# A mixture-of-experts feed-forward: the order of transposes and down products in each group

## The chip, the cores and the metric

The kernel runs on one core of a Trainium2 chip. The metric is the device time of one execution in microseconds. The kernel before takes 568.52 us, the median of three runs (567.76 to 568.71).

## The reference

The input x has shape (8, 256, 128). The first part is causal attention with 16 query heads of 8 columns and one key and value head, rotary tables, a bias, a residual and a layer norm. The second part is an RMS norm, causal attention with 16 query and 4 key heads of 64 columns, a residual, and then a mixture of experts, whose output is added and layer-normed:

```
logits = xf @ router_w + router_b
vals, idx = top_k(logits, 2);  scores = softmax(vals)
oh = one_hot(idx, 8);  pos = cumsum(cumsum(oh, axis=0), axis=1)
emask = oh * (pos < 256);  m = max over both choices of the admitted expert
h = gelu((xf @ w2[m]) * (xf @ w1[m]))        # 256 hidden columns
y = h @ w3[m]
slot = y where the choice was admitted, else xf
out = sum over the two choices of slot * scores
```

Each of the 2048 tokens so goes through one expert alone, m.

## The kernel before, in words

The batch of 8 is run as a software pipeline of steps; the last steps route the tokens. Tokens are handled in two passes: tiles 0 to 9 (five batch entries) and tiles 10 to 15. In each pass VectorE works out a slot for every token so that the tokens of an expert lie together (`slots`, L1713), GpSimd scatters the rows to `xs_dram` by indirect DMAs (`scatter`, L605) and loads the slots back as tiles of 128 rows (`load_slots`). A pass has 17 or 13 such tiles, each of one expert; they are worked in **16 groups** of two tiles (groups 8 and 15 have one). For group n:

- TensorE turns the slots into bank "xg" of the ring (`turn_slots`, L1211, recorded at L1218). ScalarE copies them to xT_a or xT_b by the group's parity (`take_slots`, L2136, recorded at L2140).
- TensorE forms both up products (`up`, L1236, recorded at L1242) into ps_st. Expert numbers are loaded to registers for two groups at a time (`find_experts`, L1223).
- ScalarE copies one half (`copy`, L2145, L2151, tile prod), VectorE multiplies it by the other (`gate`, L1750, L1756), ScalarE does the gelu (`gelu`, L2153, L2159).
- TensorE turns the gelu's rows into bank "ht" (`turn_hidden`, L1246, recorded at L1252), VectorE copies them to hidT, which the profile names pvs (`take_hidden`, L1759, L1763).
- TensorE forms the down product into bank "dn" (`down`, L1255, recorded at L1262; its w3 has the name pvb), VectorE copies it to ysb, which the profile names qkr (`take_outputs`, L1766, L1771), and SP stores that to `ys_dram` (L557).

When the stores of a pass have landed, GpSimd gathers the rows per token (`gather`, L630, recorded at L632), and VectorE adds them with their weights (`add_outputs`, L1782, recorded at L1792), forms statistics (L1799) and normalises. In the last group VectorE adds the first five tiles of the first pass right after its copies.

The groups overlap by an order written out by hand for each engine. In the loop's turn n TensorE forms the up product of n, and then, before the change, turns the gelu's rows of n-1, turns the slots of n+1 and forms the down product of n-2. VectorE gates n, copies the hidden rows of n-1 and then the outputs of n-2. ScalarE does the copy of n, the slots of n+1, the gelu of n. The routing of the second pass goes in between (`between`, both engines, by the table BETWEEN).

Four PSUM banks form a ring. `Ring.__init__` lists every use of a bank in TensorE's order; a use waits (`fill`) until the use four places earlier was emptied, and a reader waits (`filled`) until the counter `full` has reached the use's number:

```
def bank(self, step, name):
    return self.at[step, name] % self.banks
def full(self, step, name):
    return self.at[step, name] + 1
def freed(self, step, name):
    return self.at[step, name] // self.banks
```

So the list in `Ring.__init__` and TensorE's own order must agree. `down(n)` waits for `take_hidden(n)`; `turn_hidden(n)` waits for `gelu(n)`; `up(n)` waits for `take_slots(n)` and for the gate of n-2; `take_outputs(n)` waits for the down product and for the store of n-2, which has the same half of ysb.

Of the kernel before, what the change touches and what calls it, by code (L numbers as in the profile page):

```python
# [32 lines left out]
NB, T, C = 8, 256, 128  # L33
# [18 lines left out]
GROUPS = [(i, list(range(START[i] + k, START[i] + min(k + 2, COUNT[i])))) for i in range(2) for k in range(0, COUNT[i], 2)]  # L52
NG = len(GROUPS)
# [47 lines left out]
BETWEEN = {(0, 0): [(NB - 1, "xfT")], (0, 1): [(NB, "xfT"), (NB - 1, "lg"), (NB, "lg")],  # L101
           (1, 1): [(NB, "cnt1")], (2, 0): [(NB, "rk1")]}


def stages(step):

    return {x for x, a in AHEAD.items() if 0 <= step + a < NB} - ({"MA"} if step < FIRST + 4 else set())


class Ring:  # L110
# [3 lines left out]
    def __init__(self, banks):  # L114
        self.banks, self.at = banks, {}
        for step in range(FIRST, NB):
            for at, name in OPENING.get(step, []):
                self.add(at, name)
            for stage, name in ORDER if step not in OPENING else []:
                if stage in stages(step):  # L120
                    for at, n in IN_STEP.get(step, {}).get(name, [(step, name)]):
                        self.add(at, n)
        for n in range(NG + 1):
            for at, name in BETWEEN.get((n, 0), []) + [(NB, f"ht{n - 1}")] * (n > 0) \
                    + [(NB, f"xg{n + 1}")] * (n + 1 < NG) + [(NB, f"dn{n - 2}")] * (n > 1) + BETWEEN.get((n, 1), []):
                self.add(at, name)
        self.add(NB, f"dn{NG - 1}")

# [78 lines left out]
def build(nc, x, Wq, bq, Wk, bk, Wv, bv, Wo, bo, g1, g2, wq, wk, wv, wo, router_w, router_b,  # L207
          w1, w2, w3, cf, cb, out):
    with ExitStack() as ctx:
# [31 lines left out]
        down = cft[:, CF_DOWN:CF_DOWN + E]  # L241
# [219 lines left out]
        def emptied(eng, s, name):  # L461

            eng.wait_ge(free[RING.bank(s, name)], RING.freed(s, name) + 1)
# [232 lines left out]
        def _(pe):  # L696
            order = iter(RING.at)

            def fill(s, name):

                assert next(order) == (s, name)
                b, f = RING.bank(s, name), RING.freed(s, name)
                if f > 0:
                    pe.wait_ge(free[b], f)
                return ps_r[:, b, :]
# [169 lines left out]
            def turn_tokens(s):  # L875

                o = fill(s, "xfT")
                pe.wait_ge(xf_in, s)
                for t in range(NT):
                    mm = nc.tensor.transpose(o[:, P * t:P * (t + 1)], xf[:, t, :], ident)  # L880
                mm.then_inc(full, 1)
# [11 lines left out]
            def counts(part):  # L893

                lo, hi = PARTS[part]
                pe.wait_ge(oh_in, part + 1)
                fill(ROUTED[part], f"cnt{part}")
                o = counted(part)
                nc.tensor.matmul(o, tri, oh_b[:, 0:2, lo:hi, :], start=True, stop=False, skip_group_check=True)
                for i in range(hi - 1):  # L900
                    first = max(lo, i + 1)
                    mm = nc.tensor.matmul(o[:, :, first - lo:, :], cbt[:, CB_ONES:CB_ONES + P],
                                          oh_b[:, 0:2, i, :].unsqueeze(2).broadcast_to([P, 2, hi - first, E]),
                                          start=False, stop=i == hi - 2, skip_group_check=True)
                mm.then_inc(full, 1)

            def ranks(i):

                lo, hi = PASSES[i]
                pe.wait_ge(ch_in, i + 1)  # L910
                fill(ROUTED[i], f"rk{i}")
                o = ranked(i)
                nc.tensor.matmul(o[:, 0:hi - lo, :], tri, chosen[:, lo:hi, :], start=True, stop=False,
                                 skip_group_check=True)
                for k in range(lo, hi):
                    mm = nc.tensor.matmul(o[:, k - lo + 1:, :], cbt[:, CB_ONES:CB_ONES + P],
                                          chosen[:, k, :].unsqueeze(1).broadcast_to([P, hi - k, E]),
                                          start=False, stop=k == hi - 1, skip_group_check=True)
                mm.then_inc(full, 1)
# [326 lines left out]
            def turn_hidden(n, g):  # L1246

                pe.wait_ge(hid_in, n + 1)
                o = fill(NB, f"ht{n}").rearrange("p (t k c) -> p t k c", t=2, k=HK)
                for t in range(len(g)):  # L1250
                    for k in range(HK):
                        mm = nc.tensor.transpose(o[:, t, k, :], hid[:, n % 2, t, P * k:P * (k + 1)], ident)  # L1252
                mm.then_inc(full, 1)

            def down(n, g):  # L1255

                emptied(pe, NB, f"ht{n}")
                o = fill(NB, f"dn{n}")
                for t, tile in enumerate(g):
                    at = expert.pop(tile)  # L1260
                    for k in range(HK):
                        mm = nc.tensor.matmul(o[:, C * t:C * (t + 1)], hidT[:, n % 2, t, k, :],  # L1262
                                              w3_flat[:, bass.ds(at + C * k, C)], start=k == 0, stop=k == HK - 1)
                mm.then_inc(full, 1)

            def between(n, half):

                for at, name in BETWEEN.get((n, half), []):
                    if name == "cnt1":
                        counts(1)  # L1270
                    if name == "rk1":
                        ranks(1)
                    if name == "xfT":
                        turn_tokens(at)
                    if name == "lg":
                        logits(at)
# [4 lines left out]
            for n, (i, g) in enumerate(GROUPS):  # L1281
                up(n, i, g)
                if n % 2:
                    find_experts(n + 1)
                between(n, 0)
                if n > 0:
                    turn_hidden(n - 1, GROUPS[n - 1][1])
                if n + 1 < NG:
                    turn_slots(n + 1, *GROUPS[n + 1])
                if n > 1:  # L1290
                    down(n - 2, GROUPS[n - 2][1])
                between(n, 1)
            turn_hidden(NG - 1, GROUPS[NG - 1][1])
            down(NG - 2, GROUPS[NG - 2][1])
            down(NG - 1, GROUPS[NG - 1][1])


# [1 line left out]
        def _(dve):  # L1299
# [313 lines left out]
            at = [0]  # L1613
# [145 lines left out]
            def take_hidden(n, g):  # L1759

                b = filled(dve, NB, f"ht{n}")
                w = len(g) * HID
                V.tensor_copy(hidT[:, n % 2].rearrange("p t k c -> p (t k c)")[:, 0:w], ps_r[:, b, 0:w]) \  # L1763
                    .then_inc(free[b], 1)

            def take_outputs(n, g):  # L1766

                b = filled(dve, NB, f"dn{n}")
                if n > 1:
                    dve.wait_ge(ys_dma[n % 2], 16 * (n // 2))  # L1770
                V.tensor_copy(ysb[:, n % 2, 0:len(g), :], ps_r[:, b, 0:len(g) * C].rearrange("p (t c) -> p t c", c=C)) \  # L1771
                    .then_inc(free[b], 1)
# [53 lines left out]
            def between(n, half):  # L1826

                if (n, half) == (0, 1):
                    take_logits(NB - 1, NB - 2)
                    take_logits(NB, NB - 1)  # L1830
                    first_choices(1)
                if (n, half) == (1, 1):
                    admit(1)
                if (n, half) == (2, 0):
                    slots(1)
                if (n, half) == (8, 1):
                    shares(*PASSES[1], 2)
                if (n, half) == (10, 1):
                    dve.wait_ge(z_in, NB)
                    add_kept(0, 5, 1)  # L1840
                if (n, half) == (11, 1):
                    add_kept(5, 10, 1)
                if (n, half) == (12, 1):
                    add_kept(10, 16, 3)
                if (n, half) == (15, 1):
                    add_outputs(0)
# [11 lines left out]
            for n, (i, g) in enumerate(GROUPS):  # L1858
                gate(n, g)
                between(n, 0)  # L1860
                if n > 0:
                    take_hidden(n - 1, GROUPS[n - 1][1])
                if n > 1:
                    take_outputs(n - 2, GROUPS[n - 2][1])
                between(n, 1)
            take_hidden(NG - 1, GROUPS[NG - 1][1])
            take_outputs(NG - 2, GROUPS[NG - 2][1])
            statistics(0)
            take_outputs(NG - 1, GROUPS[NG - 1][1])
            add_outputs(1)  # L1870
# [337 lines left out]
```

## Time and profile before

| | |
|---|---|
| median of three runs | 568.52 us |
| the profiled execution | 569.94 us |
| its span, first to last instruction | 568.1 us |
| TensorE matmul busy | 474.3 us (83%) |
| VectorE busy | 373.4 us (66%) |
| ScalarE busy | 231.3 us (41%) |
| GpSimd busy | 161.9 us (28%) |
| mean granted TensorE clock | 0.957 of full |

The groups of the feed-forward lie between 481 and 549 us of the span; what comes after is the last store, six gathers, the sums and the final layer norm. PE is TensorE's matmul, DVE is VectorE, ACT is ScalarE, POOL is GpSimd. A busy share says little of a stage with several limits, so the timelines of the single engines are what to read here. The ends of matmuls are modelled by the profiler, and successive ones overlap; the starts give the pace.

### The profile page before, as it was taken

The page shows a single profiled execution, that of the slowest core. Times are in us where ns is not written, and L with a number is a line of the kernel's source. Part 1 is how long each engine was busy: PE and PEld are TensorE (multiplying, and loading weights), DVE is VectorE, ACT ScalarE, POOL GpSimd, SP SyncE. Part 2 cuts the span into 40 slices and gives each one's busy share as a digit, 9 for nine tenths or more (in the row PEclk, how much of TensorE's full clock was granted, in tenths as well). Part 3 has the DMA queues.
Part 4 walks back from the last instruction along what each step waited for, and adds up shares of the span by engine and source line. Part 5 has one row for each costly group of instructions (what it writes and reads, how often), then busy time and mean ns, then how long its engine had stood idle before and what let it go on. Part 6 is the DMA issues. An engine that isn't in the chain of part 4 may idle for free.

```text
span 568.1 us, 8434 instructions
## 1 busy us (share of the span) xinstructions
PE 474.3 (83%) x2980; PEld 262.4 (46%) x2980; DVE 373.4 (66%) x1023; ACT 231.3 (41%) x418; POOL 161.9 (28%) x200
## 2 busy tenths in 40 slices
PE   3877877899899999999998999899888689798730
PEld 2445443454455455536454554455436236465520
DVE  3634789667666786585867577776966136745585
ACT  1252431744554274338334642642431330545332
POOL 4311222402402243033313132232332760051612
PEclk9986999999999999999999999999988789999985
DMA  7400000000030003001100300030430350041213
GB/s 213 168 2 2 1 2 1 2 1 1 3 77 2 0 3 77 1 3 36 42 1 4 76 2 0 5 76 1 141 86 10 106 161 1 1 133 32 64 53 97
DMA packets 19095, 23.95 MB, mean 42 GB/s; under 512 B 2630, under 2 KB 15374, under 8 KB 18158
## 3 DMA queue, kind: packets, MB, share of 16 engines
q1 hardware_dynamic: 15308, 18.29, 11.9%
q0 software_dynamic: 1648, 4.07, 2.6%
q10 hardware_dynamic: 2098, 1.05, 0.6%
q8 instruction: 25, 0.41, 0.3%
q14 instruction: 16, 0.13, 0.1%
HBM read 16.81 MB, written 6.28 MB: 41 GB/s over the span
## 4 chain that ended last, share of the span: by engine, by line
PE 57%; DVE 19%; ACT 11%; issue 6%; POOL 3%; another core or an unknown queue 2%; DMA 1%; ACTq 1%; POOLq 0%; DVEq 0%
PE ps_r L997 6%; PE ps_st L962 6%; PE ps_r L867 5%; DVE rmax_a L1340 4%; ACT pt L1902 4%; PE ps_r L712 4%; PE ps_r L1024 4%; PE ps_st L1242 4%; PE ps_st L951 4%; PE ps_r L1013 3%; PE ps_r L770 3%; DVE rmax L1340 3%; PE ps_r L844 2%; POOL qkr L603 2%
## 5 line engine op out<-in xcount | busy, mean ns | idle before, releaser
L603 POOL TENSOR_TENSOR qkr<-qkr,prod 128x512 f32<-128x512 f32 (+1 forms) x48 | 52.3, 1095 | 191.6 <-DVE prod L1466 190.5
L1340 DVE TENSOR_REDUCE rmax_a<-ps_r 128x2 f32<-128x512 f32 (+1 forms) x96 | 61.2, 686 | 31.2 <-PE ps_r L844 31.0
L1340 DVE TENSOR_REDUCE rmax<-ps_r 128x2 f32<-128x512 f32 (+1 forms) x96 | 60.7, 684 | 13.5 <-PE ps_r L976 13.1
L1902 ACT ACTIVATE pt<-ps_st 128x1024 f32<-128x1024 f32 x48 | 46.5, 1022 | 54.7 <-PE ps_st L754 54.6
L712 PE MATMUL ps_r<-cbt 128*128 128x256 bf16 (+1 forms) x192 | 61.9, 323 | 4.0 <-ACT xT_b L1926 1.1
L1911 ACT ACTIVATE pt<-ps_st 128x1024 f32<-128x1024 f32 x48 | 47.3, 1022 | 37.0 <-PE ps_st L962 31.6
L997 PE MATMUL ps_r<-pt,vb 128*64 128x512 f32 x192 | 50.0, 627 | 7.7 <-issue 4.2
L640 POOL TENSOR_TENSOR oT<-pvb,oT 128x1024 f32<-128x1024 f32 x14 | 32.9, 2371 | 78.9 <-DMA oT<-inv_dram 78.9
L1024 PE MATMUL ps_r<-wqkv,xT_b 128*128 128x512 f32 x96 | 44.5, 600 | 4.3 <-DVE rmax_a L1340 3.5
L712 PEld LDWEIGHTS ps_r<-cbt 128*128 128x128 bf16 x192 | 18.6, 97 | 48.0 <-issue 34.6
L962 PE MATMUL ps_st<-qbuf,kbuf 64*128 64x512 f32 x288 | 39.8, 408 | 0.0
L844 PE MATMUL ps_r<-kq_a 128*128 128x512 f32 x84 | 39.2, 532 | 0.0
L1972 ACT ACTIVATE pvb<-ps_r 128x512 f32<-128x512 f32 x32 | 18.9, 595 | 46.7 <-PE ps_r L997 39.4
L962 PEld LDWEIGHTS ps_st<-qbuf,kbuf 64*128 64x128 f32 x288 | 25.2, 184 | 14.4 <-issue 10.2
L770 PE MATMUL ps_r<-pt,va 128*32 128x512 f32 x192 | 24.0, 601 | 7.0 <-ACT pt L1902 4.1
L1463 DVE TENSOR_TENSOR qkr<-ps_r,cft 128x512 f32<-128x512 f32 (+1 forms) x48 | 28.6, 595 | 0.3 <-PE ps_r L1024 0.2
L867 PE MATMUL ps_r<-wob,oT 128*128 128x128 f32 x224 | 28.0, 286 | 0.0
L867 PEld LDWEIGHTS ps_r<-wob,oT 128*128 128x128 f32 x224 | 27.2, 202 | 0.8 <-issue 0.8
L1478 DVE TENSOR_TENSOR qbuf<-ps_r,qbuf 128x512 fp32r<-128x512 f32 x32 | 20.7, 685 | 10.2 <-ACT qbuf L1990 10.1
L1024 PEld LDWEIGHTS ps_r<-wqkv,xT_b 128*128 128x128 f32 x96 | 17.1, 189 | 22.3 <-issue 13.8
L976 PE MATMUL ps_r<-kbuf,qbuf 128*128 128x512 f32 x64 | 26.0, 479 | 0.0
L1033 PE MATMUL ps_r<-cft,qkr 128*128 128x128 f32 x160 | 22.8, 281 | 3.4 <-DVE prod L1466 2.6
(238 smaller groups left out, 888.9 us busy)
## 6 DMA issues: line engine op xcount, KB each, us to landing
oT<-inv_dram SPq DMA_DIRECT2D x14, 512.0 KB, 5.7
xs_dram<-pvb SPq DMA_DIRECT2D x1, 2048.0 KB
pt<-in_L_ffn_w SPq DMA_DIRECT2D x2, 1024.0 KB, 7.1
ys_dram<-qkr SPq DMA_DIRECT2D x14, 128.0 KB
qkr<-xs_dram POOLq DMA_DIRECT2D x4, 256.0 KB, 7.0
x_all<-in_L_attn_x ACTq DMA_DIRECT2D x1, 896.0 KB, 7.2
pvb<-xs_dram POOLq DMA_DIRECT2D x3, 256.0 KB, 3.9
out<-x_all SPq DMA_DIRECT2D x1, 640.0 KB
```

The costliest lines, as they stand in the source:

```text
L603: nc.gpsimd.tensor_tensor(part, part, prod[:, (3 * t + i) % 2, 0:w], ALU.add).then_inc(add_in, 1)
L640: ins = nc.gpsimd.tensor_tensor(oT[:, k], pvb[1 - u][:, k, :, :].rearrange("p t (g c) -> p t g c", g=G), oT[:, k], ALU.mult)
L712: nc.tensor.matmul(o[:, :, P * (i >= 4):], ident_b, qmask.unsqueeze(1).broadcast_to([P, heads, P]), start=True, stop=False, skip_group_che ...
L770: mm = nc.tensor.matmul(o[RG * a:RG * (a + 1), :], va[n % 2][:, kt, :], pt_a(kind)[:, 4 * a:4 * a + 4, :], start=i == 0, stop=i == len(blo ...
L844: nc.tensor.matmul(o, q, k, start=False, stop=True, skip_group_check=True).then_inc(full, 1)
L867: mm = nc.tensor.matmul(o[:, 0:C], of, wob[:, j, :], start=j == 0, stop=j == H // 2 - 1)
L962: mm = nc.tensor.matmul(o[b], k, q, start=False, stop=ql, tile_position=(DB * b, 0))
L997: mm = nc.tensor.matmul(o[DB * b:DB * (b + 1), :], vb[s % 2][:, kt, hk, :], pt_b(kind)[:, G * hk:G * (hk + 1), :], start=j == 0, stop=j == ...
L1024: nc.tensor.matmul(o, xT_b[:, P * t:P * (t + 1)], wqkv[:, 512 * i:512 * (i + 1)], start=True, stop=True).then_inc(full, 1)
L1340: nc.vector.tensor_reduce(heads_of(i), ps_r[:, b, :].rearrange("p (h k) -> p h k", h=4 if i < 4 else 2), AX.X, ALU.max).then_inc(free[b], 1)
L1902: nc.scalar.activation(pt_a(kind)[:, 8 * half:8 * half + 8, :], ps_st[:, c % 2, :, :].rearrange("p b (h t) -> p (b h) t", h=4), ACT.Exp, s ...
L1911: nc.scalar.activation(pt_b(kind)[:, 8 * half:8 * half + 8, :], ps_st[:, c % 2, :, :].rearrange("p b (h t) -> p (b h) t", h=4), ACT.Exp, s ...
```

## The change

TensorE's order within a turn, VectorE's order of its two copies, and the ring's list change together. TensorE turns the next slots, forms the down product, then turns the gelu's rows; VectorE takes the outputs, then the hidden rows. After the loop, the down product of group 14 comes ahead of turning group 15's rows, and VectorE's copies likewise.

```
@@ Ring.__init__
         for n in range(NG + 1):
-            for at, name in BETWEEN.get((n, 0), []) + [(NB, f"ht{n - 1}")] * (n > 0) \
-                    + [(NB, f"xg{n + 1}")] * (n + 1 < NG) + [(NB, f"dn{n - 2}")] * (n > 1) + BETWEEN.get((n, 1), []):
+            for at, name in BETWEEN.get((n, 0), []) + [(NB, f"xg{n + 1}")] * (n + 1 < NG) \
+                    + [(NB, f"dn{n - 2}")] * (n > 1) + [(NB, f"ht{n - 1}")] * (n > 0) + BETWEEN.get((n, 1), []):
                 self.add(at, name)
@@ TensorE
                 between(n, 0)
-                if n > 0:
-                    turn_hidden(n - 1, GROUPS[n - 1][1])
                 if n + 1 < NG:
                     turn_slots(n + 1, *GROUPS[n + 1])
                 if n > 1:
                     down(n - 2, GROUPS[n - 2][1])
+                if n > 0:
+                    turn_hidden(n - 1, GROUPS[n - 1][1])
                 between(n, 1)
+            down(NG - 2, GROUPS[NG - 2][1])
             turn_hidden(NG - 1, GROUPS[NG - 1][1])
-            down(NG - 2, GROUPS[NG - 2][1])
             down(NG - 1, GROUPS[NG - 1][1])
@@ VectorE
                 between(n, 0)
+                if n > 1:
+                    take_outputs(n - 2, GROUPS[n - 2][1])
                 if n > 0:
                     take_hidden(n - 1, GROUPS[n - 1][1])
-                if n > 1:
-                    take_outputs(n - 2, GROUPS[n - 2][1])
                 between(n, 1)
+            take_outputs(NG - 2, GROUPS[NG - 2][1])
             take_hidden(NG - 1, GROUPS[NG - 1][1])
-            take_outputs(NG - 2, GROUPS[NG - 2][1])
             statistics(0)
```

## Rows read from the trace of the kernel before

**Rows 1.** The page: TensorE's part of the busy times, and its granted clock in 40 slices.
```profile
PE 474.3 (83%) x2980; PEld 262.4 (46%) x2980; DVE 373.4 (66%) x1023; ACT 231.3 (41%) x418; POOL 161.9 (28%) x200
...
PEclk9986999999999999999999999999988789999985
```

**Rows 2.** Timeline of TensorE, groups 4 and 5: start us, us, engine, line, operation [idle before].
```profile
498.40 1.88 PE L1242 MATMUL ps_st<-pt,xT_a 128*128 x4
500.12 0.60 PE L1252 MATMUL ps_r<-cft,flat 128*128 128x128 f32 x4
500.55 0.38 PE L1218 MATMUL ps_r<-cft,qkr 128*128 128x128 f32 x2
500.77 1.06 PE L1262 MATMUL ps_r<-pvb,pvs 128*128 x8
501.67 1.88 PE L1242 MATMUL ps_st<-pt,xT_b 128*128 x4
503.38 0.60 PE L1252 MATMUL ps_r<-cft,flat 128*128 128x128 f32 x4
...
504.04 1.06 PE L1262 MATMUL ps_r<-pvb,pvs 128*128 x8
505.78 1.98 PE L1242 MATMUL ps_st<-pt,xT_a 128*128 x4 [0.69 <-ACT xT_a L2140]
```

**Rows 3.** Timeline of VectorE in the same stretch.
```profile
501.55 0.68 DVE L1763 COPY pvs<-ps_r 128x512 f32<-128x512 f32 x1
504.68 0.42 DVE L1771 COPY qkr<-ps_r 128x256 f32<-128x256 f32 x1 [2.45 <-PE ps_r L1218]
```

**Rows 4.** Timeline of ScalarE in the same stretch.
```profile
501.67 0.63 ACT L2159 ACTIVATE flat<-flat 128x512 f32<-128x512 f32 x1 [0.31 <-issue]
504.76 0.60 ACT L2151 ACTIVATE prod<-ps_st 128x512 f32<-128x512 f32 x1 [2.45 <-PE ps_st L1242]
```

**Rows 5.** Timeline of GpSimd: the last scatter of the second pass.
```profile
502.50 0.96 POOL L612 DMA_INDIRECT xs_dram<-xf,sidx  x1 [0.30 <-issue]
```

**Rows 6.** Timelines of TensorE and VectorE around group 3.
```profile
495.19 0.60 PE L1252 MATMUL ps_r<-cft,flat 128*128 128x128 f32 x4
497.18 0.41 PE L1218 MATMUL ps_r<-cft,qkr 128*128 128x128 f32 x2 [1.39 <-DVE pvs L1763]
...
496.34 0.69 DVE L1763 COPY pvs<-ps_r 128x512 f32<-128x512 f32 x1
496.95 0.42 DVE L1771 COPY qkr<-ps_r 128x256 f32<-128x256 f32 x1
497.28 0.68 DVE L1756 TENSOR_TENSOR flat<-prod,ps_st 128x512 f32<-128x512 f32 x1
```

**Rows 7.** Timelines of TensorE, ScalarE, VectorE, groups 13 to 15, under the gathers.
```profile
537.34 1.98 PE L1242 MATMUL ps_st<-pt,xT_a 128*128 x4 [2.64 <-ACT xT_a L2140]
542.07 1.12 PE L1242 MATMUL ps_st<-pt,xT_b 128*128 x2 [1.31 <-ACT xT_b L2140]
...
536.80 0.39 ACT L2140 ACTIVATE xT_a<-ps_r 128x256 f32<-128x256 f32 x1 [3.03 <-remote]
...
535.39 0.69 DVE L1763 COPY pvs<-ps_r 128x512 f32<-128x512 f32 x1 [0.84 <-PE ps_r L1262]
539.70 0.42 DVE L1771 COPY qkr<-ps_r 128x256 f32<-128x256 f32 x1 [3.62 <-remote]
```

**Rows 8.** Timelines of VectorE and TensorE at the end of the groups.
```profile
543.98 0.68 DVE L1763 COPY pvs<-ps_r 128x512 f32<-128x512 f32 x1
544.77 0.42 DVE L1771 COPY qkr<-ps_r 128x256 f32<-128x256 f32 x1
545.11 1.39 DVE L1792 SCALAR_TENSOR_TENSOR x_all<-pt,kz,x_all 128x128 f32<-128x128 f32 x5
548.30 0.29 DVE L1771 COPY qkr<-ps_r 128x128 f32<-128x128 f32 x1
...
547.11 0.71 PE L1262 MATMUL ps_r<-pvb,pvs 128*128 x4 [1.15 <-DVE pvs L1763]
```

More of the change, by code:

```diff
@@ L123, in __init__ @@
         for n in range(NG + 1):
-            for at, name in BETWEEN.get((n, 0), []) + [(NB, f"ht{n - 1}")] * (n > 0) \
-                    + [(NB, f"xg{n + 1}")] * (n + 1 < NG) + [(NB, f"dn{n - 2}")] * (n > 1) + BETWEEN.get((n, 1), []):
+            for at, name in BETWEEN.get((n, 0), []) + [(NB, f"xg{n + 1}")] * (n + 1 < NG) \
+                    + [(NB, f"dn{n - 2}")] * (n > 1) + [(NB, f"ht{n - 1}")] * (n > 0) + BETWEEN.get((n, 1), []):
                 self.add(at, name)
@@ L1285, in _ @@
                 between(n, 0)
-                if n > 0:
-                    turn_hidden(n - 1, GROUPS[n - 1][1])
                 if n + 1 < NG:
@@ L1291, in _ @@
                     down(n - 2, GROUPS[n - 2][1])
+                if n > 0:
+                    turn_hidden(n - 1, GROUPS[n - 1][1])
                 between(n, 1)
+            down(NG - 2, GROUPS[NG - 2][1])
             turn_hidden(NG - 1, GROUPS[NG - 1][1])
-            down(NG - 2, GROUPS[NG - 2][1])
             down(NG - 1, GROUPS[NG - 1][1])
@@ L1860, in _ @@
                 between(n, 0)
+                if n > 1:
+                    take_outputs(n - 2, GROUPS[n - 2][1])
                 if n > 0:
                     take_hidden(n - 1, GROUPS[n - 1][1])
-                if n > 1:
-                    take_outputs(n - 2, GROUPS[n - 2][1])
                 between(n, 1)
+            take_outputs(NG - 2, GROUPS[NG - 2][1])
             take_hidden(NG - 1, GROUPS[NG - 1][1])
-            take_outputs(NG - 2, GROUPS[NG - 2][1])
             statistics(0)
```

## The prediction

> **What bounds the kernel now.** I read the page first: over the whole span TensorE is busy 474.3 us of 568.1, and its granted clock stands at the full level (2.4 GHz) in all but one of the slices that hold the feed-forward and falls only when its work is over [rows 1]. The change touches only the sixteen groups of the feed-forward, so I then read TensorE's timeline there. Group 4 is a clean one [rows 2]: the up product starts at 498.40, turning the gelu's rows ("ht") at 500.12, turning the next slots ("xg") at 500.55, the down product ("dn") at 500.77, and the next up product at 501.67. Start to start that is 1.72 + 0.43 + 0.22 + 0.90 = 3.27 us, with no gap. TensorE sets the pace, and anything else counts only where it makes TensorE wait.
>
> The last rows of [rows 2] show such a place. The down product recorded at 504.04 would have let the next up product start at 504.94, and it starts at 505.78 after a wait for ScalarE's copy of the turned slots. The rows of VectorE and ScalarE [rows 3, 4] tell more: VectorE takes the output of group 2 at 504.68, though its down product ran at 500.77 to 501.67, and ScalarE takes the up product of group 5 at 504.76, though that one began at 501.67 and its successor at 503.38. So TensorE's completion signals reached nobody from about 501.8 to 504.65. GpSimd was then at its scatters through indirect DMAs [rows 5]. I call this a **hold-up**. A second one stands at 534 to 541, under the gathers [rows 7]: TensorE waits 2.64 us and 1.31 us, VectorE sits 3.62 us ahead of taking an output.
>
> **The change part by part.** No instruction is added or removed. DMAs are the same in number; the store of each group's output is issued about 0.6 us earlier against its group, since VectorE's copy of outputs now goes ahead of its 0.60 us copy of hidden rows.
>
> *Clean groups: 0.* The cover must be checked on two chains. Before, the tight one is gelu to ht: the gelu of group 4 ends at 501.67 + 0.63 = 502.30 and its ht starts at 503.38 [rows 2, 4], 1.1 us of slack. The change gives that chain xg and dn as well, 1.1 us more: a gain of slack that no clean group needs. The other chain is ht, VectorE's copy into hidT, dn. Before, ht of group n-1 is followed by xg, dn, up, ht and xg ahead of its own dn: 0.22 + 0.90 + 1.72 + 0.43 + 0.22 = 3.5 us. After, only up and xg lie between, 1.94 us. Against the group's start, VectorE's gate starts at 2.55 (500.95, which is 501.55 less its 0.60), the outputs' copy at 3.15, the hidden copy at 3.15 + 0.33 = 3.48, and ends 0.68 later at 4.16. The dn wants it at 3.27 + 1.94 = 5.21. With 0.14 us for the signal, 0.9 us of slack remain. The copy of slots on ScalarE is bound by the copy of the up product ahead of it, so an earlier xg speeds no up product. The ring of four banks moves too: ht now waits for the outputs three groups back, xg for the hidden rows three back; both are long taken.
>
> *Group 3, +0.55.* Here VectorE is late, since it makes the second pass's slots. Before, ht of group 2 runs at 495.19, then xg waits 1.39 us for the ring bank which VectorE's hidden copy of 496.34 frees [rows 6]; behind the wait come xg and dn. After, xg goes in front, dn of group 1 waits for the same hidden copy, which now stands behind the outputs' copy (0.33 more), and behind the wait come dn and ht. So +0.33 + (0.43 - 0.22) = +0.55 us.
>
> *First hold-up, +1.49 in all.* I take it to lie at the same clock time, as the scatters hang on VectorE's slot numbers and not on the changed order. Before, VectorE did the hidden copy at 501.55 and then was caught in the outputs' copy at 504.68 [rows 3], which nobody on TensorE needed. After, the outputs' copy is caught first and **the hidden copy is queued behind it**: 504.68 + 0.33 = 505.01, ending 505.69; dn of group 3, due at about 504.2, can start at 505.69 + 0.14 = 505.83. Then dn 0.90, ht 0.43 and 0.11 for starting from rest (495.19 to 498.40 holds such a 0.11: 497.18 to 498.40 is 1.22 for 1.12 of work), so the up product of group 6 starts at 507.27 rather than 505.78. That takes in the 0.55 of group 3. Bounds: if the signals are not held there, the up product comes at 498.95 + 2 x 3.27 = 505.49, which is -0.29; if they are held past that, each us costs one.
>
> *Second hold-up, 0, between -1.4 and +2.* It follows the gathers, whose start shifts with the rest. Signals come one by one. After the up product of group 13 the first signal was ht's, at 535.39 by VectorE's row, the next xg's, at 536.80 by ScalarE's row [rows 7]. With xg first, the up product of group 14 could start 1.4 us sooner. But the third signal, 539.70, is then ht's: hidden copy to 540.4, dn of group 12 at 540.5 and ht to 541.9, while the up product of group 15 waits as before for a signal until 542.07. So the 1.4 is given back.
>
> *The end, +0.5.* Before, TensorE ran ht and dn back to back, and VectorE took th 14 at 543.98, outputs 13 at 544.77, then the sums of 545.11 [rows 8]. After, group 14's hidden copy of group 13 is 0.33 later, ending 543.40, dn of group 13 starts at 543.54, ht of group 14 ends at 544.9, and its hidden copy runs 545.0 to 545.6: the sums start 0.5 us later, then the remaining copies, statistics and the last output (548.30) with them. The last store and gathers hang on that one. TensorE's former wait of 1.15 us at 547.11 goes, but VectorE is the bound there; its bounds are +0.2 (hidden copy of 13 not late) and +0.6.
>
> *Sum.* 1.49 + 0 + 0.5 = +2.0 us. The profiled execution took 569.94 us (span 568.1 and 1.8 around it), which would become 571.9. It lies 1.4 above the median 568.52, on which the prediction stands: 570.5 us. The measurement can tell about 0.2%, 1.14 us.
>
> **A rule against this reading.** The rows show TensorE's signals late while GpSimd makes indirect DMAs [rows 3, 5]. The Trainium skill, in "SBUF — State Buffer", section "Who interferes with whom", says that DMA never contends with a compute engine and that only the port pair of VectorE and GpSimd is shared. By it the hold-ups would have no cause in the scatters and need not come again at those places; the time would be that of the first rival. The trace speaks against taking it so, though it doesn't show what holds the signals.
>
> **The rivals.**
> *The hold-up misses the new short chain.* For it: the signals between 496 and 501 came on time under the same scatters. Then the part up to group 6 gives -0.29 to +0.55, the end +0.2 to +0.5: between 568.4 and 569.6, no measurable change. 0.30.
> *Faster: the slots' signal gets out first.* The mechanism stands in group 13: xg's signal takes the place of ht's and the up product of group 14 starts at 535.9. It decides if the signals behind it come less than 2 us apart, so that dn of group 12 is ready in time. With the first hold-up missed (-0.29) and +0.2 at the end: 568.52 - 0.29 - 1.4 + 0.2 = 567.0; with the second wait of 1.31 gone too, 565.7. Against it: nothing sets the third signal free sooner. 0.23.
> *Slower by more.* Both hold-ups catch the hidden copy; the second costs up to 2 us as well: 572.5. 0.07.
> The forecast itself has 0.40.
>
> **How the numbers follow.** Slower by over 0.2%: 0.40 + 0.07 = 0.47. Same: 0.30. Faster: 0.23. The forecast's own range is 569.7 to 571.9. The range for 8 in 10 takes in the rival without change and most of the faster one: 566.8 to 572.2.
>
> **What would show it.** Right: in group 3 TensorE waits about 1.7 to 2.1 us ahead of dn (now a wait for hidT, pvs by name); near 504 a second wait of dn for pvs, where none stands now; VectorE's outputs' copy directly ahead of a late hidden copy; the sums of 545.11 later against the last up product. Clean groups still 3.27 us. Wrong: no wait of dn in group 5; clean groups at another pace; fewer or shorter waits of the up product for the turned slots, which would mean that the early xg pays.

## The result, and the profile after

The changed kernel is slower: 570.76 us, the median of 20 runs (567.9 to 574.47), against 567.76 us for the kernel before in 20 runs of its own. The ratio is 1.007 with a 95% interval of [1.005, 1.0091], so 3 to 4 us (3.0 by medians, 3.7 by means). A second measurement (after_again, below) gave 1.0043 [1.0012, 1.0075]. Ratios and mean times, here and below, leave out the few executions that took over 1.5% longer than the fastest of their kernel. The direction and the order of the size were forecast (+2.0 us); a part of the cost, something like half by the estimates below, has a cause that the forecast didn't have.

Here is TensorE's timeline of the changed kernel, as [rows 2, 6, 7, 8] show it before.

```profile
484.12 3.40 PE L1242 MATMUL ps_st<-pt,xT_b 128*128 x4
...
494.20 0.38 PE L1218 MATMUL ps_r<-cft,qkr 128*128 128x128 f32 x2
496.25 1.15 PE L1262 MATMUL ps_r<-pvb,pvs 128*128 x8 [1.67 <-DVE pvs L1763]
497.24 0.60 PE L1252 MATMUL ps_r<-cft,flat 128*128 128x128 f32 x4
497.68 1.88 PE L1242 MATMUL ps_st<-pt,xT_a 128*128 x4
...
504.25 1.15 PE L1262 MATMUL ps_r<-pvb,pvs 128*128 x8 [1.21 <-DVE pvs L1763]
505.24 0.60 PE L1252 MATMUL ps_r<-cft,flat 128*128 128x128 f32 x4
505.68 1.88 PE L1242 MATMUL ps_st<-pt,xT_a 128*128 x4
...
535.09 1.98 PE L1242 MATMUL ps_st<-pt,xT_a 128*128 x4 [0.36 <-ACT xT_a L2140]
536.91 0.27 PE L1218 MATMUL ps_r<-cft,pvb 128*128 128x128 f32 x1
539.75 1.15 PE L1262 MATMUL ps_r<-pvb,pvs 128*128 x8 [2.58 <-issue]
...
545.24 1.15 PE L1262 MATMUL ps_r<-pvb,pvs 128*128 x8 [0.87 <-DVE pvs L1763]
```

The wait of group 3 has moved from xg to dn and grown from 1.39 us [rows 6] to 1.67. In group 5 dn waits 1.21 us for the hidden rows where no such wait stood. In group 13 the up product of group 14 waits 0.36 us and not 2.64 [rows 7], since the slots' signal came first, but dn in group 14's turn then waits 2.58. The profile names no releaser for that wait; the hidden copy that this dn needs started at 538.93 on VectorE (below) and ended at 539.62, 0.13 us ahead of it. Near the end dn waits again.

VectorE's timeline of the same kernel, to be held against [rows 3, 6, 8]:

```profile
495.08 0.42 DVE L1771 COPY qkr<-ps_r 128x256 f32<-128x256 f32 x1
495.43 0.68 DVE L1763 COPY pvs<-ps_r 128x512 f32<-128x512 f32 x1
...
501.93 0.42 DVE L1771 COPY qkr<-ps_r 128x256 f32<-128x256 f32 x1 [1.01 <-PE ps_r L1252]
503.42 0.69 DVE L1763 COPY pvs<-ps_r 128x512 f32<-128x512 f32 x1 [1.07 <-PE ps_r L1218]
...
538.18 0.42 DVE L1771 COPY qkr<-ps_r 128x256 f32<-128x256 f32 x1 [3.25 <-PE ps_r L1218]
538.93 0.69 DVE L1763 COPY pvs<-ps_r 128x512 f32<-128x512 f32 x1 [0.33 <-remote]
...
545.01 1.39 DVE L1792 SCALAR_TENSOR_TENSOR x_all<-pt,kz,x_all 128x128 f32<-128x128 f32 x5
...
548.24 0.29 DVE L1771 COPY qkr<-ps_r 128x128 f32<-128x128 f32 x1
```

At 495 the hidden copy stands 0.35 us behind the outputs' copy. At 501.93 and 503.42 both are late, and at 538.18 and 538.93 again.

The first row of the TensorE fence shows a thing that the forecast didn't have: an up product of four matmuls took 3.40 us instead of 1.96. The table by stretches says why (columns: stretch, its length, busy us of PE, PEld, DVE, ACT and POOL, the granted TensorE clock as a share of full, the DMA engines' busy share, GB/s):

```profile
480.00:483.60 3.60, 2.02 (x16) 1.46 (x15) 2.38 (x11) 2.14 (x7) 0.00 (x0) 1.00 0.00 0
483.60:487.00 3.40, 3.40 (x10) 1.85 (x10) 2.32 (x12) 1.59 (x2) 0.00 (x0) 0.50 0.00 0
```

From 483.6 to 487.0 TensorE had half its clock, 1.2 GHz for 2.4, after a stretch in which it had been busy 2.02 us of 3.60. No such stretch lies in the feed-forward of the profile of before. But this one is not the change's doing: TensorE's order is the same in both kernels up to this up product, and in the profile of before the same stretch of work, with the same 2.02 us of 3.60, is followed by the full clock:

```profile
482.09:485.69 3.60, 2.02 (x16) 1.46 (x15) 2.37 (x11) 2.16 (x7) 0.00 (x0) 1.00 0.00 0
485.69:489.09 3.40, 2.90 (x16) 1.66 (x15) 2.52 (x13) 2.57 (x4) 0.00 (x0) 1.00 0.00 0
```

Six of the 14 profiles of this case have half the clock at this place (changed, after_again, filled_again, after_filled, best, slots_first), and best has TensorE's order of before. It comes in some executions and not in others. Here it cost some 1.1 us: from the first up product to that of group 3 the changed kernel took 13.78 us for 12.69.

Each execution also records its mean granted clock, and the kernels can be compared by it. One stretch of 3.4 us at half clock in a span of 568 us lowers that mean by 0.5 x 3.4 / 568 = 0.003.

### The profile page after: what moved, and what is told of

Same layout as the page of the kernel before. It is cut to its first block and busy times, and to the rows that moved or that the text cites. A ratio compares the mean times of both kernels' runs of the same rounds, so it can differ in the third digit from the quotient of the medians.

```text
span 568.3 us, 8433 instructions
## 1 busy us (share of the span) xinstructions
PE 471.4 (83%) x2980; PEld 260.3 (46%) x2980; DVE 374.2 (66%) x1023; ACT 230.5 (41%) x418; POOL 161.4 (28%) x200
## 5 line engine op out<-in xcount | busy, mean ns | idle before, releaser
L844 PE MATMUL ps_r<-kq_a 128*128 128x512 f32 x84 | 37.7, 512 | 0.0
L867 PE MATMUL ps_r<-wob,oT 128*128 128x128 f32 x224 | 26.3, 276 | 0.0
L867 PEld LDWEIGHTS ps_r<-wob,oT 128*128 128x128 f32 x224 | 25.6, 192 | 0.8 <-issue 0.8
```

The source lines that it names most:

```text
L844: nc.tensor.matmul(o, q, k, start=False, stop=True, skip_group_check=True).then_inc(full, 1)
L867: mm = nc.tensor.matmul(o[:, 0:C], of, wob[:, j, :], start=j == 0, stop=j == H // 2 - 1)
```

## The experiments

The kernels of the experiments were run on three chips (B, C, D), each with the kernel before beside it. Chips differ (before: 564.4, 555.6 and 567.5 us by median), so only ratios on one chip are compared. The changed kernel itself was run on D alone of the three (after_again); the rows of before and changed in the second table are those of the first pair of profiles, whose chip is not on record. The first table gives times and mean clocks, the second the time from one up product's start to the next, read from TensorE's timelines of one profiled execution each.

| kernel | chip | ratio to before | 95% interval | mean us | mean clock, with its standard error |
|---|---|---|---|---|---|
| before | B | | | 564.21 | 0.9620 ± 0.0007 |
| tensor_only | B | 1.0049 | 1.0015 to 1.0083 | 566.92 | 0.9590 ± 0.0016 |
| vector_only | B | 1.0044 | 1.0011 to 1.0077 | 566.14 | 0.9611 ± 0.0012 |
| before_quiet | B | 0.9948 | 0.9923 to 0.9972 | 561.31 | 0.9620 ± 0.0011 |
| after_quiet | B | 1.002 | 0.9995 to 1.0045 | 565.17 | 0.9575 ± 0.0013 |
| before | C | | | 555.79 | 0.9648 ± 0.0006 |
| after_filled | C | 1.0006 | 0.9974 to 1.0039 | 556.18 | 0.9660 ± 0.0010 |
| after_quiet_filled | C | 1.0 | 0.9968 to 1.0032 | 556.21 | 0.9661 ± 0.0009 |
| end_old | C | 1.0027 | 0.999 to 1.0064 | 557.20 | 0.9638 ± 0.0013 |
| slots_first | C | 0.9981 | 0.9946 to 1.0017 | 554.74 | 0.9645 ± 0.0012 |
| before | D | | | 567.09 | 0.9600 ± 0.0007 |
| after_again | D | 1.0043 | 1.0012 to 1.0075 | 570.27 | 0.9584 ± 0.0010 |
| filled_again | D | 1.0021 | 0.9988 to 1.0053 | 568.41 | 0.9601 ± 0.0016 |
| best | D | 1.0017 | 0.9984 to 1.0049 | 568.50 | 0.9588 ± 0.0013 |
| end_first | D | 0.9985 | 0.9952 to 1.0018 | 566.64 | 0.9601 ± 0.0017 |

| us, one profile each | group 3 | group 4 | group 5 | 13 and 14 | last up to last output's copy |
|---|---|---|---|---|---|
| before | 4.92 | 3.27 | 4.12 | 10.93 | 6.24 |
| changed | 5.19 | 3.27 | 4.74 | 10.48 | 6.93 |
| after_again | 5.19 | 3.27 | 4.97 | 10.41 | 6.50 |
| before_quiet | 4.91 | 3.27 | 3.30 | 6.55 | 5.94 |
| after_quiet | 5.45 | 4.96 | 3.27 | 6.47 | 6.61 |
| tensor_only | 5.12 | 3.27 | 3.69 | 7.22 | 10.72 |
| vector_only | 5.31 | 3.27 | 3.56 | 7.43 | 6.83 |
| after_filled | 5.49 | 3.27 | 3.27 | 6.47 | 6.61 |
| after_quiet_filled | 5.45 | 3.27 | 3.27 | 6.46 | 6.61 |
| filled_again | 5.19 | 3.68 | 4.78 | 7.85 | 6.63 |
| end_old | 6.56 | 3.82 | 3.27 | 6.47 | 5.94 |
| slots_first | 4.89 | 3.27 | 3.27 | 6.43 | 5.93 |
| best | 3.27 | 3.42 | 5.60 | 10.55 | 6.01 |
| end_first | 5.06 | 3.27 | 3.96 | 8.20 | 5.04 |

**Without the indirect DMAs in the groups.** Both kernels were run with the second pass's scatters and the first pass's gathers taken out:

```
@@ GpSimd, both kernels
-            scatter(1, lo, hi - NT, xf_all[:, lo:, :])
-            scatter(1, hi - NT, hi, xf)
+            pool.wait_ge(sc_in, 2)
...
-            for k in range(*PASSES[0]):
-                if k > 1:
-                    pool.wait_ge(yg_even_odd[k % 2], 16 * (k // 2))
-                gather(k, 0, yg_even_odd[k % 2])
@@ VectorE, add_outputs: no wait for yg_even_odd
```

> The kernel before without the scatters of the second pass and without the gathers of the first, so GpSimd makes no indirect DMA while the groups run. Left out: the tokens of the second pass reach no expert, and the first pass's sums take what lies in their buffer. Theory (signals of TensorE are held up by these DMAs): no wait of the up product for turned slots at group 6, 14 or 15, the groups shorter by some 4 us, time 562 to 565 (0.99 to 0.995). Rival (the hold-ups have another cause, for instance the loading of expert numbers at groups 5 and 13): the waits stay, time within 0.3% of before.

> The changed kernel with the same left out as in before_quiet. Theory (the change costs through hold-ups, 0.55 us in group 3 and some tenths at the end): against before_quiet only 0.7 to 1.1 us (0.1 to 0.2%), and waits of L1262 for pvs only in group 3 and in the last two groups. Rival (the new order costs in clean groups): still 3 to 4 us over before_quiet, with clean groups over 3.27 us from up product to up product.

The first held: the waits of groups 5, 13 and 14 are gone and the time falls by 2.9 us in the mean. The groups took 3.30 and 6.55 us, for 4.12 and 10.93 in the profile of before, which may be of another chip; on chip B itself the two profiles that have these DMAs, tensor_only and vector_only, show 3.69 and 3.56 in group 5 and 7.22 and 7.43 in 13 and 14. That TensorE's completion signals come late under GpSimd's indirect DMAs, and on time without them, is so shown for this chip by four profiles. How much of the 2.9 us is due to the hold-ups is not shown: the extra of those two profiles is about 0.4 and 0.9 us, and the kernel leaves out VectorE's wait for the gathered rows as well. On chip C, no profile has the hold-ups even with the DMAs in place (after_filled, end_old and slots_first, all 3.27 in group 5); why is open.

The second missed by both theories. After_quiet is not 0.7 to 1.1 but 3.9 us over before_quiet (565.17 - 561.31, standard error 0.7), as much as the changed kernel lies over before with the DMAs in place (3.7 us in the first pair, 3.2 on chip D). So the hold-ups are not what makes the change slow. And its clean groups are 3.27. Between before_quiet and after_quiet the time from the first up product to the last output's copy grew by 2.88 us (61.79 to 64.68), in three places: group 3 by 0.54, the end by 0.67, and group 4 by 1.69. The rows of TensorE of after_quiet:

```profile
493.20 1.15 PE L1257 MATMUL ps_r<-pvb,pvs 128*128 x8 [1.92 <-DVE pvs L1758]
494.19 0.60 PE L1247 MATMUL ps_r<-cft,flat 128*128 128x128 f32 x4
494.62 3.58 PE L1237 MATMUL ps_st<-pt,xT_a 128*128 x4
497.99 0.43 PE L1213 MATMUL ps_r<-cft,qkr 128*128 128x128 f32 x2
```

and its table by stretches:

```profile
490.89:494.62 3.73, 1.81 (x15) 1.57 (x14) 2.82 (x10) 1.50 (x3) 2.81 (x4) 1.00 0.45 136
494.70:498.10 3.40, 3.40 (x6) 1.23 (x6) 0.80 (x2) 0.00 (x0) 0.00 (x0) 0.50 0.54 171
498.10:502.85 4.75, 4.75 (x33) 3.74 (x32) 2.33 (x5) 2.37 (x5) 0.00 (x0) 1.00 0.10 30
```

The wait of group 3, now 1.92 us for 1.37, was followed by half the clock from 494.7 to 498.1. In the same place before_quiet keeps its pace:

```profile
494.41 0.41 PE L1213 MATMUL ps_r<-cft,qkr 128*128 128x128 f32 x2 [1.37 <-DVE pvs L1758]
494.66 1.13 PE L1257 MATMUL ps_r<-pvb,pvs 128*128 x8
495.63 1.88 PE L1237 MATMUL ps_st<-pt,xT_a 128*128 x4
```

The mean clocks of the 12 runs of each agree: 0.9575 for 0.9620. The 0.0045 (± 0.0017) between them is one and a half such stretches, and one costs up to 1.7 us when TensorE is at work in it: up to 2.5 us, beside the 1.2 us of the two waits. That is near the 3.9, but as an upper bound with an error of 1 us. Another estimate goes by how a run's time falls with its own mean clock: 0.35 and 0.31 us per 0.001 over the 12 runs of each kernel, so 1.5 us for the 0.0045. By it about 1 us has no cause here, which is about the error of these sums.

**Which engine's order.** The changed kernel with VectorE's old order, and the kernel before with VectorE's new one:

```
@@ tensor_only: VectorE as before, in turn n and after the loop
+                    take_hidden(n - 1, ...)
                     take_outputs(n - 2, ...)
-                    take_hidden(n - 1, ...)
@@ vector_only: VectorE as changed, TensorE and Ring as before
```

> TensorE's order is the new one, VectorE copies hidden rows ahead of outputs as before. Theory (the cost comes from the short way from turning the gelu's rows to their down product, which is TensorE's order): nearly the whole cost stays, 1.005 to 1.008 of before, and the profile shows waits of L1262 for pvs in group 3 (1.4 us) and at least once more under the scatters or gathers, 3 to 5 us in sum. Rival (VectorE's queue is the cause: a late outputs' copy holds up the hidden copy behind it): the cost falls to under 1.003, and waits of L1262 for pvs outside group 3 vanish.

> TensorE's order is that of before, VectorE copies outputs first. Theory (TensorE's short way is the cause): no cost, 0.998 to 1.002, waits of L1262 for pvs at most 1 us in sum beside the one at the end. Rival (VectorE's queue is the cause): the outputs' copy caught by a late signal holds the hidden copy, waits of L1262 for pvs of 1 us or more under the scatters, 1.003 to 1.008.

My theory blamed TensorE's order alone, and that fell: each half costs by itself (1.0049 and 1.0044). Which costs more can't be told, and the two sum to more than the whole change. The rival was right on the time of vector_only and wrong on its course: dn never waits for the hidden rows under the scatters or gathers, but only twice at the end. The waits of tensor_only and then of vector_only (us in total, times, longest):

```profile
PE ps_r L1262 <- DVE pvs L1763: 6.3, 5, 2.6
```

```profile
PE ps_r L1262 <- DVE pvs L1763: 2.0, 2, 1.0
PE ps_r L1218 <- DVE pvs L1763: 1.7, 1, 1.7
```

In vector_only the wait of xg in group 3 is 1.7 us for 1.39 [rows 6], the 0.33 of the outputs' copy ahead, and the end is 6.83 for 6.24 in before (5.94 where nothing is held up): the hidden rows of group 14 are ready and stand behind an outputs' copy that waits for the down product of group 13. In tensor_only the end took 10.72 us. The late signal of the gathers caught the hidden copy here (VectorE waited 3.04 us for it), and dn behind it:

```profile
537.66 1.15 PE L1262 MATMUL ps_r<-pvb,pvs 128*128 x8 [2.65 <-DVE pvs L1763]
```

A part of the rest ran at half clock:

```profile
536.00:539.00 3.00, 1.34 (x12) 1.35 (x12) 1.35 (x3) 1.16 (x3) 0.26 (x1) 1.00 0.18 45
539.00:545.00 6.00, 4.08 (x17) 3.04 (x15) 4.35 (x16) 0.93 (x1) 0.00 (x0) 0.50 0.19 54
```

**Filling the wait of group 3.** This tests the clock by itself: TensorE is given work that nobody reads, in the wait that the change lengthened. The kernel before with the same filling was not run, so what filling gives without the change is not known.

```
@@ turn_slots, after its then_inc
+                if n == 4:
+                    pe.wait_ge(prod_e, n - 1)
+                    for _ in range(15):
+                        nc.tensor.transpose(ps_st[:, n % 2, 0, 0:P], ident, ident)
```

> The changed kernel, where TensorE fills its wait in group 3 with 15 transposes that nobody reads (1.65 us), ahead of the down product that waits for the hidden rows. Theory (half of the cost is TensorE's granted clock: its longer waits let stretches of 3.4 us fall to the half clock more often): mean granted clock of the runs rises from some 0.958 to that of before (0.961 or more), and the time falls to 1.001 to 1.004 of before, though work was added. Rival (the cost is the waits themselves): time as the changed kernel or up to 0.2 us over it, 1.005 to 1.009, clock unchanged.

> The same filling in the changed kernel without indirect DMAs in the groups (after_quiet leaves out the same). Clock theory: mean clock 0.961 or more (after_quiet had 0.9575), time 1.5 to 2.5 us under after_quiet's distance to before: ratio to before 0.996 to 0.999. Rival: 1.001 to 1.004, as after_quiet (1.002).

```profile
486.75 1.80 PE L1223 MATMUL ps_st<-cft 128*128 128x128 f32 x15
488.88 1.15 PE L1266 MATMUL ps_r<-pvb,pvs 128*128 x8 [0.33 <-DVE pvs L1767]
489.87 0.60 PE L1256 MATMUL ps_r<-cft,flat 128*128 128x128 f32 x4
490.31 1.88 PE L1246 MATMUL ps_st<-pt,xT_a 128*128 x4
```

The rows of after_filled show dn starting when VectorE lets it, group 3 as long as in after_quiet (5.49 and 5.45 us), and the up product behind it at full clock. Nothing else was changed, and the kernel is as fast as before (1.0006). It holds for after_quiet_filled too, though its ratio of 1.0 is above the 0.996 to 0.999 expected: on this chip there are no hold-ups for which leaving out the DMAs could pay. That both clocks are over 0.961 says little, since before has 0.9648 on this chip; they lie 0.001 above it, about one standard error. The changed kernel itself had not been run on chip C, so both were run on D:

> The changed kernel once more, on one chip with its filled form. Clock theory: 1.004 to 1.008 of before, mean granted clock 0.002 to 0.004 under before's. Rival (the chip, not the filling, made the filled form as fast as before): 0.999 to 1.003 here too, and clock as before.

> The changed kernel with 15 unread transposes in TensorE's wait of group 3, as in after_filled. Clock theory: 0.999 to 1.003 of before, 1.5 us or more under after_again, clock at before's level or over. Rival: within 0.5 us of after_again.

Filling took 1.9 us off the mean (570.27 to 568.41, standard error 0.9) and the clock rose from 0.9584 to 0.9601. Each clock difference on chip D is about its standard error; together with the times on two chips, and with after_quiet, they point one way. The profiles do too: behind group 3's wait the clock halved in the two where that wait was over 1.9 us and not filled (after_quiet, end_old), in none of the three filled ones and in none where it was 1.30 to 1.70 us. So the clock is supported as a cause by several weak signs, not settled by one. With 1.2 us of waits left in it, the filled kernel should be near 1.002, and it is at 1.0006 and 1.0021.

After_again also shows the first hold-up taking the course that was forecast, on VectorE:

```profile
504.32 0.42 DVE L1771 COPY qkr<-ps_r 128x256 f32<-128x256 f32 x1 [2.40 <-PE ps_r L1218]
504.66 0.68 DVE L1763 COPY pvs<-ps_r 128x512 f32<-128x512 f32 x1
```

and on TensorE:

```profile
505.49 1.15 PE L1262 MATMUL ps_r<-pvb,pvs 128*128 x8 [1.44 <-DVE pvs L1763]
```

**The end with its old order.** Turn 15 and what follows the loop as before on both engines, the rest as changed.

```
@@ TensorE, turn 15 and after the loop (Ring and VectorE to match)
+                if n == NG - 1:
+                    turn_hidden(n - 1, GROUPS[n - 1][1])
                 down(n - 2, ...)
...
+            turn_hidden(NG - 1, GROUPS[NG - 1][1])
             down(NG - 2, GROUPS[NG - 2][1])
-            turn_hidden(NG - 1, GROUPS[NG - 1][1])
```

> The changed kernel, but the last turn and what follows it have the order of before on both engines. Theory: 0.5 to 0.7 us under the changed kernel, 1.004 to 1.008 of before; in the profile from the start of the last up product to VectorE's last copy of outputs 5.9 us rather than 6.6 to 6.9. Rival (the end costs nothing, since VectorE bounds it): that stretch stays at 6.6 or more.

The end is back at 5.94 us, 0.67 less, as expected. The ratio 1.0027 lies below the expected range, but can't be told from it or from 1. Its profile caught another half-clock stretch behind the wait of group 3 (6.56 us for the group):

```profile
491.42 1.89 PE L1264 MATMUL ps_r<-pvb,pvs 128*128 x8 [1.93 <-DVE pvs L1767]
```

```profile
487.40:491.60 4.20, 2.27 (x9) 1.03 (x8) 3.79 (x17) 1.24 (x3) 1.38 (x2) 1.00 0.01 4
491.60:495.10 3.50, 3.50 (x14) 2.98 (x14) 1.39 (x3) 0.63 (x1) 2.62 (x3) 0.51 0.43 124
```

**Only the slots first.** The kernel before with xg ahead of ht, dn last.

```
@@ TensorE and Ring
-                turn_hidden(n - 1, ...)
                 turn_slots(n + 1, ...)
+                turn_hidden(n - 1, ...)
                 down(n - 2, ...)
```

> The kernel before with only the turning of the next slots moved ahead of turning the gelu's rows; the down product stays last and VectorE's order is that of before. Theory (the harm is in the short way from ht to its down product and the wait of dn behind it; early slots gain nothing in clean groups): 0.998 to 1.002. Faster rival (early slots' signal pays under the hold-ups): 0.994 to 0.997. In group 3 the wait moves from xg to dn, of 1.0 to 1.6 us.

0.9981 [0.9946, 1.0017]: no cost, and no gain that can be told. Dn waits for the hidden rows in group 3 as expected (1.30 us), but ht now runs ahead of the wait, as it did before the change, so the group stays at 4.89. The faster rival could not show itself, as the profiles of this chip have no hold-ups.

**Two moves on VectorE.** They go after the two waits that bound both kernels.

```
@@ best and end_first, VectorE, order of before
-                if (n, half) == (15, 1):
-                    add_outputs(0)
...
-            statistics(0)
             take_outputs(NG - 1, GROUPS[NG - 1][1])
+            add_outputs(0)
+            statistics(0)
@@ best alone: in turn 2, take_hidden(1), then slots(1), then take_outputs(0)
```

> The order of before, with two moves on VectorE: in turn 2 the hidden rows of group 1 are copied ahead of working out the second pass's slots, and at the end the last copies of hidden rows and outputs go ahead of the sums and statistics of the first five tiles. Theory (TensorE's waits in group 3 and at the end are VectorE's queue): the wait of group 3 (1.4 us) falls under 0.3, the last output is copied 4.2 to 4.6 us after the start of the last up product rather than 5.9, in all 2.5 to 3.2 us less, more with the clock: 0.992 to 0.996. Rival (the slots, 0.6 us later, hold the gate of group 3 and the scatters, and the sums return behind the gathers): 0.997 to 1.001.

> The order of before with the second move of best alone (last copies ahead of sums and statistics). Theory: 1.3 to 1.7 us less, 0.996 to 0.998; wait of group 3 unchanged. Rival (the sums return on the way behind the gathers): 0.999 to 1.001, with the last copy earlier and VectorE's wait for the gathered rows gone.

In best the wait of group 3 is gone (3.27 us for 4.92), and given back two groups later. TensorE and then GpSimd:

```profile
506.80 1.98 PE L1242 MATMUL ps_st<-pt,xT_a 128*128 x4 [2.17 <-ACT xT_a L2142]
```

```profile
506.79 2.87 POOL L620 DMA_DIRECT2D pvb<-xs_dram  x4 [1.82 <-DMA xs_dram<-xf,sidx]
```

The up product of group 6 waits for the slots' copy, whose signal comes only at the end of the hold-up: 2.17 us for 0.69 [rows 2]. Counted from the start of group 3's up product it starts at 12.28 us, for 12.30 before, so the gain of group 3 is gone. The last scatter starts at 504.01 for 502.50 [rows 5]; of these 1.5 us 1.04 were lost ahead of group 3, behind another half-clock stretch in group 1, and only some 0.5 are the later slot numbers. The hold-up would have eaten most of the gain even so, since TensorE merely waited longer for the same signal. The last output was to be copied 4.2 to 4.6 us after the last up product, and it took 6.01: from 543.6 to 547.0 the clock stood at 0.53. The ratio is 1.0017 [0.9984, 1.0049]: the theory's 0.992 to 0.996 is ruled out, the rival's 0.997 to 1.001 is not. End_first shortened the end to 5.04 us, of which VectorE waited 0.69 us for an earlier store of ysb, and took away VectorE's wait for the gathered rows (1.97 us in before), but its 0.9985 [0.9952, 1.0018] is not clear of no change. No version run here is shown to beat the kernel before.

## Why the prediction was right, and where it was short

- **Clean groups, 0: right.** 3.27 us in groups 4, 6 and 12 of the changed kernel, and in after_quiet. The slack of 0.9 us on ht, hidden copy, dn was enough.
- **Group 3, +0.55: right.** 4.91 to 5.45 in the pair without DMAs. In the changed kernel's own profile it is 5.19, as in after_again and filled_again, which have the same half-clock stretch in group 1. That this made TensorE later against VectorE is argued and not shown; after_filled has such a stretch too, and 5.49.
- **First hold-up, +1.49 in all: mechanism right, size too large, and less important than I made it.** Groups 3 to 5 took 12.31 us before, 13.20 and 13.43 in the two profiles after: +0.9 and +1.1. Dn waited for pvs as forecast (1.21 and 1.44 us). But the change costs as much where the hold-ups are removed.
- **Second hold-up, 0: right, with its course.** Groups 13 and 14 went from 10.93 to 10.48 and 10.41. The early slots' signal was gained (0.36 for 2.64 us) and given back behind (2.58).
- **The end, +0.5: right.** 0.67 in the quiet pair, 0.69 in the first, and 0.26 in after_again (6.50 for 6.24).
- **The clock, absent from the forecast.** This is what the sum lacked. I read in [rows 1] that the clock was full in the groups and took it to stay so. A wait of TensorE was costed at its length alone. The granted clock can halve behind it for 3.4 us, which costs up to 1.7 us more, in some executions and not in others. That is some 1.5 to 2.5 us of the mean difference, by the clocks of the quiet pair and by filling the wait, each with an error of about 1 us.
- **The sum.** Forecast +2.0, measured 3.0 by medians, 2.8 to 5.2 by the interval. The profiled pair differs by 2.0 from first up product to last output's copy (67.52 to 69.54 us), which agrees with the forecast's figure by luck: 1.1 us of it was lost to half the clock ahead of anything that the change moved, and the hold-ups cost less than forecast. As whole executions the two took 569.94 and 570.07 us, as the changed kernel reached its first up product 2.1 us sooner; one profile of each says little of a difference of 3 us. The 570.5 lies near the measured 570.76 since the base of 20 runs was 0.8 us lower than that of three.
- **The rule of the Trainium skill** that DMA never contends with a compute engine ("SBUF — State Buffer", "Who interferes with whom") would have had no hold-ups. The runs on chip B decide against using it so: TensorE's completion signals came late in the two profiles with these DMAs and not in the two without. What they contend for no run shows; the rule is about SBUF ports, and may hold for those.

## What to carry to other kernels

Ask of a reordering what it puts behind each wait and how long the wait becomes, on every engine: here both halves, TensorE's and VectorE's, lengthened the same two waits. Where an engine's granted clock can fall behind a wait, a wait of 1.9 us for 1.4 can cost more than the half us between them, so compare the mean granted clock over many executions and not the one profile. Before a stall or a slow stretch in the profile of the changed kernel is put down to the change, look whether the instructions ahead of it were changed at all: the half clock in group 1 was not the change's. A stall removed ahead of a fixed event (here the landing of the scatters) is returned there; look for that event first.

## What the hardware showed that I had not expected

- TensorE was granted half its clock for 3.4 us after stretches in which it had been busy about half of the time (2.02 us of 3.60 in the changed kernel, 1.81 of 3.73 in after_quiet, 2.27 of 4.20 in end_old), with no single wait over 1.93 us in these three. The Trainium skill ("TensorE: Matmul & The Clock Gate", in the table of its section "Why this matters for your kernels") warns of long idle gaps; these traces show that waits of under 2 us can be followed by the half clock. In other profiles the same was not: group 3 with 1.67 us in the changed kernel kept the full clock, and so did the kernel before behind the same 2.02 us of 3.60.
- Fifteen transposes that nobody reads made a kernel faster by 1.9 us in the mean on one chip, with a standard error of 0.9.
- Completion signals of TensorE came late under GpSimd's indirect DMAs (a down product that ended at 501.67 was taken at 504.68 [rows 2, 3], and VectorE sat 3.62 us under the gathers [rows 7]) on chips B and D and in the first pair of profiles, and not in the three profiles of chip C that have these DMAs; the runs of the kernel before were also 1.5 to 2% faster on that chip than on the other two.
